# One softmax's maxima, the products of the sums and the result of an earlier quad turned by a single transpose

## What is computed

```
q, k = rope(x @ Wq), rope(x @ Wk)          # 32 score heads of width 8
v    = x @ Wv                              # 16 heads of width 16
probs = softmax(q k^T / sqrt(8))           # 1024 x 1024 for each of 32 heads
w    = probs[:, :, 0] - lam * probs[:, :, 1]
attn = w @ v
attn = attn * rsqrt(mean(attn^2) + 1e-5) * subln_g * (1 - LAMBDA_INIT)
```

## Time and profile before

| what | value |
|---|---|
| median of 3 executions | 6013.19 us (6007.52 to 6013.4) |
| the profiled execution's own time | 6007.5 us |
| its span in the profile | 6005.7 us |
| TensorE busy (matmul) | 5596.6 us, 93% |
| VectorE busy | 5494.2 us, 91% |
| ScalarE busy | 4976.1 us, 83% |
| GpSimd busy | 2065.5 us, 34% |

### The profile page before, as it was taken

One profiled execution on the slowest core, in us unless ns is written; L12 is line 12 of the kernel. 1 busy time (PEld: TensorE's weight loads), 2 busy tenths in 40 slices (PEclk: granted clock), 3 DMA queues, 4 the chain that ended last, 5 costly groups with the idle time before them and its releaser, 6 DMA issues. The chain is left out here.

```text
span 6005.7 us, 167689 instructions
## 1 busy us (share of the span) xinstructions
PE 5596.6 (93%) x50896; PEld 1965.7 (33%) x50896; DVE 5494.2 (91%) x6072; ACT 4976.1 (83%) x9206; POOL 2065.5 (34%) x3655
## 2 busy tenths in 40 slices
PE   8878999999999999999999999999999999987775
PEld 4541333333333333333333333333333333325423
DVE  7868999999999999999999999999999999957706
ACT  6665999999999999999999999999999999973304
POOL 7981222222222222222222222222222222236406
PEclk9997999999999999999999999999999999998878
DMA  5671222322222223222322232222232222215598
GB/s 178 204 204 50 52 52 52 52 52 52 52 52 52 53 52 52 53 51 51 54 50 52 52 52 51 51 52 51 51 52 52 52 52 52 52 43 194 177 366 270
DMA packets 469606, 495.27 MB, mean 82 GB/s; under 512 B 132051, under 2 KB 330867, under 8 KB 468963
## 3 DMA queue, kind: packets, MB, share of 16 engines
q1 hardware_dynamic: 467939, 485.74, 34.3%
q10 hardware_dynamic: 1024, 0.53, 0.0%
HBM read 360.60 MB, written 123.21 MB: 81 GB/s over the span
## 5 line engine op out<-in xcount | busy, mean ns | idle before, releaser
L741 DVE TENSOR_REDUCE at_largest<-at_ps_m 128x1 f32<-128x1024 f32 x4096 | 4694.1, 1208 | 46.9 <-PE at_ps_m L845 35.2
L707 ACT ACTIVATE at_e<-at_ps_e 128x512 f32<-128x512 f32 x8192 | 4407.7, 598 | 357.7 <-PE at_ps_e L814 157.5
L831 PE MATMUL at_ps_o<-at_e,at_v 128*32 128x256 f32 (+1 forms) x30720 | 2680.4, 421 | 35.2 <-ACT at_e L707 25.3
L845 PE MATMUL at_ps_m<-k_stack,q_stack 48*128 48x512 bf16 x8192 | 2484.8, 384 | 87.9 <-DVE at_largest L741 55.5
L814 PE MATMUL at_ps_e<-q_stack,k_stack 51*128 51x512 bf16 x8192 | 2515.2, 382 | 7.7 <-issue 2.1
L831 PEld LDWEIGHTS at_ps_o<-at_e,at_v 128*32 128x32 f32 x30720 | 844.9, 149 | 1559.5 <-issue 818.4
L814 PEld LDWEIGHTS at_ps_e<-q_stack,k_stack 51*128 51x128 bf16 x8192 | 568.6, 93 | 1665.8 <-ACT at_e L707 1628.2
L626 POOL TENSOR_TENSOR at_negated<-at_zeros,at_largest_t 128x32 f32<-128x32 f32 x256 | 64.7, 253 | 2169.4 <-DVE at_largest_t L748 2169.4
L845 PEld LDWEIGHTS at_ps_m<-k_stack,q_stack 48*128 48x128 bf16 x8192 | 574.7, 93 | 219.5 <-DVE at_largest L741 188.8
L669 POOL TENSOR_TENSOR at_rms<-at_mean_eps,at_minus_half 128x16 f32<-128x16 f32 x128 | 372.6, 2911 | 10.0
L645 POOL TENSOR_TENSOR at_crossed<-at_totals 128x32 f32<-128x32 f32 x128 | 32.2, 252 | 760.9 <-DMA at_totals<-at_sums 760.9
(11 more groups left out here) (132 smaller groups left out, 3003.0 us busy)
## 6 DMA issues: line engine op xcount, KB each, us to landing
k_stack<-k_parts SPq DMA_DIRECT2D x1536, 64.0 KB
q_stack<-q_parts SPq DMA_DIRECT2D x256, 192.0 KB
q_stack<-q_parts SPq DMA_DIRECT2D x256, 128.0 KB
w_first<-in_w SPq DMA_DIRECT2D x32, 1024.0 KB, 11.7
ex_w_second<-in_w SPq DMA_DIRECT2D x32, 1024.0 KB, 12.7
q_parts<-pr_parts SPq DMA_DIRECT2D x96, 256.0 KB, 2.5
k_parts<-pr_parts SPq DMA_DIRECT2D x96, 256.0 KB, 2.8
pr_x_in<-in_x SPq DMA_DIRECT2D x16, 1024.0 KB, 6.0
```

The costliest lines, as they stand in the source:

```text
L707: nc.scalar.activation(e[:, j % E_BUFS], ps_e[:, bank(u, j)], ACT.Exp, scale=SCALE).then_inc(exp_done, 1)
L741: nc.vector.reduce_max(largest[:, u % 2, j // SIDE, j % SIDE:j % SIDE + 1], ps_m[:, j % 2], AX.X).then_inc(max_done, 1)
L831: last = nc.tensor.matmul(ps_o[32 * tile:32 * tile + 32, columns], v[:, u, tile // 2, first:first + 2 * VD * TILES - kt:TILES], e[:, (QUAD ...
L845: last = nc.tensor.matmul(ps_m[:, j % 2, half * HALF:(half + 1) * HALF], q_stack[rows, u, pair, c, t * P:(t + 1) * P], k_stack[rows, u, pa ...
```

## The change

The products (columns 0 to 543), the result of an earlier quad (544 to 799) and the maxima of the softmax c = 0 (800 to 831) lie side by side in one tile, `upright`. One transpose of 128x832 at g = 8 writes `turned`, in place of those at g = 5, g = 8 and g = 11. The maxima of c = 1 keep a tile and a transpose of their own at g = 0. Ahead of the large transpose VectorE waits for five things, four of these waits on small instructions that only increment a semaphore. GpSimd's `finish` is cut in two: `cross` makes the products early in a quad, `finish` comes behind the split of the maxima of c = 0. The result of a quad goes out one quad later, and SyncE's stores move with it. The first quad has a large transpose too, and the last result a transpose of its own. The diff, cut to its core:

```diff
+        OUT_COL, LARGEST_COL, TURN_COLS = HALF + BLK, HALF + BLK + HALF // 2, HALF + BLK + HALF // 2 + BLK
         loops = quads // BUFS - 1
-        PE_HEAD, ACT_HEAD, DVE_HEAD = 200, 144, 192
+        PE_HEAD, ACT_HEAD, DVE_HEAD = 200, 144, 184
...
-            largest, largest_t = sb("largest", [P, 2, 2, BLK]), sb("largest_t", [P, BLK])
+            upright, turned = sb("upright", [P, TURN_COLS]), sb("turned", [P, TURN_COLS])
+            largest1, largest1_t = sb("largest1", [P, BLK]), sb("largest1_t", [P, BLK])
...
+            crossed, crossed_t = upright[:, 0:OUT_COL], turned[:, 0:OUT_COL]
+            attn_t = upright[:, OUT_COL:LARGEST_COL].rearrange("p (b s v) -> p b s v", s=2, v=VD)
+            out = turned[:, OUT_COL:LARGEST_COL]
+            largest0, largest0_t = upright[:, LARGEST_COL:], turned[:, LARGEST_COL:]
...
-                def store(n, u):
-                    sp.wait_ge(out_done, n + 1)
+                def store(n):
+
+                    sp.wait_ge(all_turned, n + 4)
                     for g in range(QUAD):
                         rows = self.attn_scr[bass.ds(2 * VD * n + VD * (g // 2), VD)]
                         columns = rows[:, (g % 2) * HALF:(g % 2 + 1) * HALF]
                         sp.dma_start(columns.rearrange("v (s c) -> s v c", s=2),
-                                     out[32 * g:32 * g + 32, u % 2]).then_inc(out_stored[u % 2], 16)
+                                     out[32 * g:32 * g + 32]).then_inc(out_stored, 16)
...
+                        second_half(n, k % BUFS, True, True)
+                        first_half(n + 1, (k + 1) % BUFS, True)
+                        store(n - 1)
...
+                def split(m, c, base):
+
+                    pool.wait_ge(max1_turned if c else all_turned, m + 1)
+                    maxima = (largest1_t if c else largest0_t)
...
-                def finish(n, base):
-
+                def cross(n):
 
                     pool.wait_ge(sums_read, 2 * n + 2 + 1)
-                    if not (isinstance(n, int) and n == 0):
-                        pool.wait_ge(sums_turned, n)
+                    pool.sem_inc(pool_passed, 1)
+                    pool.wait_ge(all_turned, n + 2)
                     nc.gpsimd.tensor_tensor(crossed[:, 0:HALF], sums[:, 0], sums[:, 1], ALU.mult).then_inc(crossed_done, 1)
                     pool.wait_ge(totals_moved, 16 * TOTAL_DMAS * (n + 1))
                     nc.gpsimd.tensor_tensor(crossed[:, HALF:], totals[:, 0], totals[:, 1], ALU.mult).then_inc(crossed_done, 1)
 
-                    pool.wait_ge(sums_turned, n + 1)
+                def finish(n, base):
+
+
+                    pool.wait_ge(all_turned, n + 3)
...
+                def turn(n, base):
+
+                    cross(n - 1)
+                    split(n + AHEAD, 0, base)
+                    finish(n - 1, base + SPLIT_STEPS)
+                    split(n + AHEAD, 1, base + SPLIT_STEPS + FINISH_STEPS)
...
+                def maximum(m, j):
                     dve.wait_ge(tries_done, TRIES * m + j + 1)
-                    nc.vector.reduce_max(largest[:, u % 2, j // SIDE, j % SIDE:j % SIDE + 1], ps_m[:, j % 2], AX.X).then_inc(max_done, 1)
-
-                def turn_maxima(m, u, c):
-
-                    dve.wait_ge(max_done, TRIES * m + SIDE * (c + 1) + 2)
-                    if not (isinstance(m, int) and m == 0 and c == 0):
-                        dve.wait_ge(split_done, 2 * m + c)
-                    nc.vector.transpose(largest_t[:], largest[:, u % 2, c]).then_inc(max_turned, 1)
-
-                def turn_sums(n):
-
-                    dve.wait_ge(crossed_done, 2 * (n + 1) + 2)
-                    nc.vector.transpose(crossed_t[:], crossed[:]).then_inc(sums_turned, 1)
-
-                def turn_out(n, u):
+                    maxima = (largest1 if j // SIDE else largest0)
+                    nc.vector.reduce_max(maxima[:, j % SIDE:j % SIDE + 1], ps_m[:, j % 2], AX.X).then_inc(max_done, 1)
+
+                def turn_maxima1(m):
+
+                    dve.wait_ge(max_done, TRIES * (m + 1) + 2)
+                    if not (isinstance(m, int) and m == 0):
+                        dve.wait_ge(split_done, 2 * m)
+                    nc.vector.transpose(largest1_t[:], largest1[:]).then_inc(max1_turned, 1)
+
+                def turn_all(n, tries):
+
+                    if tries:
+                        dve.wait_ge(max_done, TRIES * (n + 1) + SIDE + 2)
+                        dve.sem_inc(dve_passed, 1)
+                        dve.wait_ge(split_done, 2 * n + 1)
+                    dve.sem_inc(dve_passed, 1)
+                    dve.wait_ge(crossed_done, 2 * n + 2)
+                    dve.sem_inc(dve_passed, 1)
                     dve.wait_ge(attn_done, n + 1)
-                    dve.wait_ge(out_stored[u % 2], 16 * QUAD * ((n + 2 - u % 2) // 2))
-                    nc.vector.transpose(out[:, u % 2], attn_t[:].rearrange("p b s v -> p (b s v)")).then_inc(out_done, 1)
-
-                def period(n, u, g, tries, rows=True, last_quad=True, this_quad=True):
+                    dve.sem_inc(dve_passed, 1)
+                    dve.wait_ge(out_stored, 16 * QUAD * (n + 1))
+                    nc.vector.transpose(turned[:], upright[:]).then_inc(all_turned, 1)
+
+                def period(n, g, tries, rows=True):
+                    if g == 0 and tries:
+                        dve.wait_ge(all_turned, n + 1)
+                    if g == TILES and tries:
+                        dve.wait_ge(max1_turned, n + 1)
                     if tries:
-                        maximum(n + AHEAD, u + AHEAD, 2 * g)
+                        maximum(n + AHEAD, 2 * g)
                     if g == 0 and rows:
-                        turn_maxima(n, u, 1)
-                    if g == TILES and tries:
-                        turn_maxima(n + 1, u + 1, 0)
-                    if g == TURN_SUMS and last_quad:
-                        turn_sums(n - 1)
-                    if g == TURN_OUT and last_quad:
-                        turn_out(n - 1, u - 1)
+                        turn_maxima1(n)
+                    if g == TILES:
...
+                        turn_all(n, tries)
                     if tries:
-                        maximum(n + AHEAD, u + AHEAD, 2 * g + 1)
+                        maximum(n + AHEAD, 2 * g + 1)
...
+                dve.wait_ge(attn_done, quads + 2)
+                dve.sem_inc(dve_passed, 1)
+                dve.wait_ge(out_stored, 16 * QUAD * (quads + 2))
+                nc.vector.transpose(out, upright[:, OUT_COL:LARGEST_COL]).then_inc(all_turned, 1)
```

More of the change, by code:

```diff
@@ L596, in _ @@
                 first_half(0, 0, True)
[L597 to L610, removed]
+                second_half(0, 0, True, True)
+                first_half(1, 1, True)
+                with hinted(nc, sp, 0, loops - 1) as i:
+                    for k in range(1, BUFS + 1):
+                        n = BUFS * i + k
+                        second_half(n, k % BUFS, True, True)
+                        first_half(n + 1, (k + 1) % BUFS, True)
+                        store(n - 1)
+                for n in range(BUFS * (loops - 1) + 1, quads):
+                    second_half(n, n % BUFS, n + AHEAD < quads, n + BUFS < quads)
+                    if n + 1 < quads:
+                        first_half(n + 1, (n + 1) % BUFS, n + 1 + AHEAD < quads)
+                    store(n - 1)
+                store(quads - 1)
+                sp.wait_ge(out_stored, 16 * QUAD * (3 + quads))
             @block.gpsimd
@@ L616, in _ @@
                 nc.gpsimd.memset(totals[:], 1.0).then_inc(ones_set, 1)
+                nc.gpsimd.memset(upright[:, 0:LARGEST_COL], 0.0).then_inc(ones_set, 1)
                 pool.sem_inc(crossed_done, 2)
@@ L621, in _ @@
                 pool.wait_ge(ones_set, ONES)
[L623 to L629, removed]
+                def split(m, c, base):
+                    pool.wait_ge(max1_turned if c else all_turned, m + 1)
+                    maxima = (largest1_t if c else largest0_t)
+                    nc.gpsimd.tensor_tensor(negated[:], zeros[:], maxima[:], ALU.subtract).then_inc(pool_step, 1)
+                    if not (isinstance(m, int) and m == 0 and c == 0):
+                        pool.wait_ge(max_stored, 16 * (P // BLK) * (2 * m + c))
+                    nc.gpsimd.tensor_tensor(parts[:, 0], zeros[:], maxima[:], ALU.subtract).then_inc(pool_step, 1)
                     pool.wait_ge(pool_step, base + 2)
@@ L675, in finish @@
                                             ALU.mult).then_inc(attn_done, 1)
[L677 to L685, removed]
-                pool.wait_ge(lam_done, 1)
[L687 to L693, removed]
+                def turn(n, base):
[3 more added lines that the diff above has]
+                    split(n + AHEAD, 1, base + SPLIT_STEPS + FINISH_STEPS)
+                for m in range(2):
+                    for c in range(2):
+                        split(m, c, SPLIT_STEPS * (2 * m + c))
+                pool.wait_ge(lam_done, 1)
```

(25 more changed lines are left out.)

37 lines of the change are left out of this document (17 added, 20 removed).

## The result

The changed kernel takes 6026.6 us (median of 7, 6013.4 to 6038.1) against 6007.5 for the kernel before (median of 7, 6002.1 to 6013.4): ratio 1.0033, 95% interval 1.002 to 1.0047. It is slower by 19 us (0.3%), where +16 us was forecast.

What follows compares the result with a forecast made beforehand. TensorE's pace plus halts bound the attention: 36.38 + 0.31 + 1.03 = 37.72 us a quad against 37.65; with loop turns +0.12 over about 126 quads, +15, head and tail +1: +16, 6030. Range 6002 to 6062, without rivals 6018 to 6042.

Steps and rivals of the forecast that it cites:

- TensorE's halts: Three halts a quad in the kernel before, 0.30, 0.52 and 0.46 us, on top of 36.38 us for 32 tries.
- The cost of the large transpose: 128x832 at g = 8: 0.96 us from its start to the next reduce, against 1.13 for the three transposes before.
- The walk at g = 8 to 10: Timed from reduce 16: try 20 can start at 4.48, reduce 21 at 6.71; TensorE's halt is 1.03 us instead of 0.52.
- g = 2 won: At the copy of the sums at g = 2, TensorE's halt falls from 0.46 to 0.31 us: 0.15 won.
- the halt behind the products: TensorE's halt of 0.30 us behind the transpose at g = 5 goes, as nothing is turned there any more.
- Waits hidden: Waits ahead of the large transpose, four of them 0.6 us, end by 0.7, within the 1.14 us after reduce 16 starts: nothing.
- rival 3: Waits ahead of the large transpose show: 0.2 to 0.7 us enter the halt at g = 8, 6055 to 6118; chance 0.12.
- GpSimd's new order: The split into `cross` and `finish` costs nothing: `finish` ends near 3045.7, ahead of g = 0 at 3053.96.
- The average: Mean quad, loop turns included: 37.93 us now, 38.05 after; +0.12 for each of about 126 quads, +15 us.
- The turn: Where TensorE's loop turns it loses 1.33 us; today 0.15 of that is won back at the next g = 2, afterwards nothing.
- Rival 1: VectorE's work decides: 0.17 us a quad less work over 126 quads saves 21 us, 5991; chance 0.12.
- Rival 2: The copy hides more of the halt at g = 10, about 0.9: 37.6 a quad, no change, 6014; chance 0.14.

Runs made afterwards that it cites:

- e5: Changed kernel plus an unused 128x256 transpose in every quad at g = 1, between reduces of try 2 and 3: quad 37.73 us, ratio 1.0036 to the kernel before.
- e6: Changed kernel plus an unused 128x256 transpose in every quad at g = 5, between reduces of try 10 and 11: quad 38.01 us, ratio 1.0135 to the kernel before.
- e4: Changed kernel with four more pairs of a wait and an increment ahead of the large transpose: quad 37.83 us, ratio 1.0075 to the kernel before.
- e9: Changed kernel with nothing joined: first maxima turned at g = 8, products behind try 18, result behind try 2; quad 37.33 us, ratio 0.9936 to the kernel before.
- e10: Changed kernel with products and maxima turned together behind try 18, result alone behind try 2 of the next quad: 37.28 us, ratio 0.992 to the kernel before.
- e1: Changed kernel with its large transpose moved from between reduces 16 and 17 to between 18 and 19: quad 37.42 us, ratio 0.9958 to the kernel before.

## Why the prediction was right

- **TensorE's halts bound the quad, not VectorE's share.** Right for the changed kernel, and shown by e5 and e6: the same work costs 0.01 or 0.29 us.
- **The cost of the large transpose.** 0.96 forecast, 0.96 measured; the rule that it starts 1.14 after reduce 16, 1.13 measured.
- **The walk at g = 8 to 10.** A halt of 1.03; four scores in 3.29 us make 3.29 - 2.27 = 1.02.
- **g = 2 won, and the halt behind the products gone.** 2.58 us for four scores, as in the quad of the earlier trace rows.
- **Waits hidden.** Right in the changed kernel; e4 shows that 0.1 us beyond the cover enters one for one, as rival 3 priced it. GpSimd's new order held nothing up either: ahead of the large transpose VectorE was idle for 0.0 us over 100 of them (1200 to 5000 us).
- **The average.** +0.12 a quad forecast, +0.12 measured over 121 quads (38.05 forecast, 38.02 measured; 37.93 taken for the kernel before, 37.90 measured, since the 123 gaps of the earlier trace rows take in the quad where the loops end, 41.3 us long). How it is made up was partly luck. The forecast put +0.07 on each ordinary quad and +0.22 on the one where TensorE's loop turns; measured are +0.11 and +0.13. Ordinary quads cost more than the walk says because of the third one of a round, and because the 37.65 of the earlier trace rows is the longest of today's three. The turn costs less: it adds 1.09 to an ordinary quad after the change and 1.07 before, where 1.33 and 1.18 were put in from the one turn of the earlier trace rows. Hardly anything was won back there today, so hardly anything was lost. The two errors cancel.
- **The time.** 6030 forecast, 6026.6 measured. The change was put 3 us too low and the time of today 5.7 too high (6013.2 of three executions, 6007.5 of seven), which partly cancel too. By its own terms (a halt of 0.96 to 1.15 over 126 quads) the forecast's range would be 6021 to 6045, not 6018 to 6042. The 3 us are below what the runs resolve.
- **Rival 1, VectorE's work decides.** It fell in the changed kernel. Its price, however, is real where the places are good: in e9 and e10 VectorE hardly waits, and one transpose fewer is worth 0.05 us a quad. The rule of the Trainium skill in "VectorE: DVE Perf Modes" (rules for kernel authors: fewer operations in a chain) holds for that case and gave the wrong sign for this one (ratio 1.0033).
- **Rival 2, the copy hides more.** It fell: the halt was not 0.9 but 1.02. What does let the copy hide a part of it is the place behind reduce 18 (e1).
- What the prediction did not see is that the change's loss was only one of place. Its own walk would have said so, tried one period later.

## What to carry to other kernels

When two engines are tied by a short ring of buffers, measure how late one may be before the other halts (here 0.34 us), and where the other halts anyway (here at each copy of the sums). Put the bulky extra work just ahead of such a copy; there joining operations saves their fixed cost. Anywhere else one long operation can cost more than several short ones, since everything above the free lateness halts the partner, and an average of busy time shows none of it.

## What the runs showed of the hardware that was not expected

- Small instructions on VectorE's queue ahead of a transpose run while the reduce before it does. A pair of a wait and an increment took 0.19 us with a register operation and 0.11 without; five waits (four of them with an increment) behind a reduce of 1.13 us delayed nothing, four more pairs delayed the transpose by 0.1.
- Lateness that stays under the free amount is not lost but carried: with a pace of 1.137 against 1.13 us it needs dozens of tries to wear off, and it turned up half a quad later in e1 (0.43 instead of 0.31).
- A halt of TensorE can cost more than its own length. In e6 the granted clock fell to 0.50 for 3.4 us in 11 quads, each 1.55 us longer, with the same halts in the quads where it did not fall.
- At the loops' end the clock fell to 0.50 in both traced executions of the changed kernel, for 3.4 us in one and for 3.4 and 10.2 in the other.
